# GpSimd waits for VectorE's routing pieces at three rows of each batch of a fused Mamba and mixture-of-experts kernel

## The chip, the cores and the metric

One Trainium2 chip, one core of it. The metric is the device time of one execution in microseconds; several executions are run and the median counts. Lower is better. All arithmetic is float32.

## What is computed

Eight sequences (batches) of 512 tokens with 512 channels go through one Mamba block and then one routed feed-forward layer, each with a residual sum and a layer norm.

```python
xz = einsum('bld,ed->bel', h, in_proj_w)             # 2048 channels: x, z
x = silu(causal_conv4(x) + conv_b)
dt, B, C = split(x_proj(x))                          # rank 32, 16 states, 16 states
delta = softplus(dt @ dt_proj_w.T + dt_proj_b)
state = state * exp(delta * A) + delta * B * x       # over 512 tokens, 1024 x 16 states
y = (sum(state * C) + x * D) * silu(z)
x1 = layernorm(h + y @ out_proj_w.T)

logits = x1 @ gate_w.T                               # 8 experts
top_vals, top_idx = top_k(logits, 2)
w = softmax(top_vals)
out = layernorm(x1 + sum_k w_k * (expert_w[top_idx_k] @ x1 + expert_b[top_idx_k]))
```

## The kernel before

The state of one batch is 16 states times 8 groups of 128 channels, so 128 **rows**, each a scan over 512 tokens. Row `step` is state `n = step // 8` and channel group `j = step % 8`. For each row ScalarE computes the decay `exp(delta*A)` (L1562, `dA`), GpSimd computes the input term `u*B` (L1691, a 128x512 product, written to `hst` or, for `j < 2`, to `first_dbu`), and VectorE scans over both (L1742). After the scans of a state TensorE transposes it (L1152, `hTp`), and VectorE adds it, weighted by C, to `y` (L1731, called a state part here, one before most even rows).

All other work of the layer is cut into named **pieces** and woven between the rows: projections (`x`, `z`, `xproj`, `dt`, `out`), the gather, the routing and the experts of the batch before, and the preparation of the next batch. The function `plan` places each piece in a row of each engine, from costs and due times, when the program is built; the result is a fixed instruction order for each engine, and semaphores hold the engines to each other's results. The batches use these plans: `SEG_PRO` for batch 0, `SEG_TWO` for batch 1, `SEG_FULL` for batches 2 to 6, `SEG_EPI` (scans in halves) for batch 7, and `SEG_LAST` behind it.

The routing of a batch has three pieces on VectorE, all built from small operations:

- `gate` (L1808 to L1823): copy the logits from PSUM, `max` and `max_index` for each of four token tiles, `gap` (L1817, the difference of the two best logits, 128x4), `hit` (L1819) and `hits` (L1823). `hits_ready` rises at its end; `gap_ready` lets ScalarE compute `eg` (L1516).
- `place` (L1838 to L1861): from TensorE's `count` (L1287, L1289, sums over `hits`), the slot of each token and the expert of each tile. `place_ready` rises at its end.
- `route` (L1868 to L1879): the two weights and the matrix `wt`. `wt_ready` rises at its end.

In `SEG_FULL` VectorE has `gate` behind the scan of row 63, `place` behind row 66 and `route` behind row 67; `x0`, `x1`, `x2` (the convolution, L1762, three operations each) follow from row 70 on. GpSimd has, behind its products, `gather1` of tile 3 at row 63, `z4` at row 65, `z5` at 67, `z6` at 70, `z7` at 73 (L1648, each waits for ScalarE's `side`, L1465), the part that is added by a DMA at row 75 (L1668), and `sig0` with `scatter0` at row 75. ScalarE has `eg` at row 65, ahead of `z6`. In `SEG_TWO` the three are behind rows 54, 55 and 56 of VectorE, and GpSimd has `sig0` (L1635) at row 57, `sig1` at 58, `sig2` at 59, three scatters (L1614) at row 60. ScalarE's `sig2` reuses the buffer that GpSimd's `sig0` reads.

GpSimd's product of row r waits for nothing of VectorE but the buffer: for `j < 2` the scan of row r-8, for `j = 2` the transposes of the state before last.

Of the kernel before, what the change touches and what calls it, by code (L numbers as in the profile page):

```python
# [32 lines left out]
ALL_TILES = TILES + HALF_TILES  # L33
LAST_LATE = ALL_TILES - 8
BANKS = 2
SLOTS = 17
USES_BANK = ("z", "zb", "moeL", "den", "countF", "biasF", "out", "outF", "gate", "gateF", "wTF", "count", "wT", "bias", "moe", "x", "xproj", "Ct", "dt")
TURNED = ("yT", "x1T", "xsT", "xsL", "yinit", "yTF", "x1TF")
# [194 lines left out]
def plan(pieces, steps, pace, weave=False):  # L233
# [16 lines left out]
    def ended(x, e, delay=0):  # L250
        if x[0] == "row":
            return not steps or added.get(x[1], 1e9) + delay <= now
        return x[0] not in MAIN and (x, e) not in exists or done.get((x, e), 1e9) + delay <= now
# [44 lines left out]
    def may_start(x):  # L298
# [5 lines left out]
        if x[0] in ("logits", "logF") and x[1] % PAIR:  # L304
            return True
        return len(users) < BANKS or ended((RELEASE[users[-BANKS][0]][0],) + users[-BANKS][1:], RELEASE[users[-BANKS][0]][1], 0.1)

# [56 lines left out]
class Segment:  # L364

    def __init__(self, pieces, pace, blocks, next_blocks, steps=STEPS):
# [10 lines left out]
        self.turned_by = [sum(row < k for row in self.turned_at.values()) for k in range(steps or 1)]  # L377
        assert len(self.use) % BANKS == 0
        self.uses = len(self.use) // BANKS
        self.blocks = blocks + [[] for _ in range(SLOTS - len(blocks))]  # L380
        self.loads = [len(x) for x in self.blocks]
        self.place = {x: (s, k) for s in range(SLOTS) for k, x in enumerate(self.blocks[s])}
        self.after = {x: (self.blocks[s] + next_blocks[s:s + 1])[k + 1:k + 2] for x, (s, k) in self.place.items()}
# [4 lines left out]
def experts(s, tiles):  # L388
    return [("We", k) for k in range(s, tiles, 3)]
# [5 lines left out]
W_FULL = [W_L[s] + W_TWO[s] for s in range(2)]  # L395
KEPT_IN = [[("Wd", e) for e in KEPT if KEPT_SLOTS[e] == s] for s in range(SLOTS)]
W_EPI = [W_L[s] + experts(s, LAST_LATE) for s in range(2)]
W_LATE = [[("Wl", k) for k in range(LAST_LATE, ALL_TILES) if k % 3 == s] for s in range(3)]
GAP = [[]] * 10
GONE_SLOTS = dict(zip(GONE, (10, 11, 4, 5, 8, 9)))  # L400
W_LAST = [W_LATE[min(s, 2)] if s in (0, 1, 14) else [("Wd", e) for e in GONE if GONE_SLOTS[e] == s] for s in range(SLOTS)]

# [80 lines left out]
class When:  # L483
# [13 lines left out]
    def bank(self, piece):  # L497

        k = self.seg.use[piece]
        return k % BANKS, self.bank_base + k // BANKS + 1  # L500

# [38 lines left out]
def periods(engine, period, last):  # L540

    def when(b, segs, before):

        return When({-1: SEG_FIRST, 0: SEG_PRO, 1: SEG_TWO, NB - 1: SEG_EPI, NB: SEG_LAST}.get(b, SEG_FULL), b, b % 2, sum(x.uses for x in segs), sum(len(x.turned) for x in segs),
                    [sum(x.loads[s] for x in segs) for s in range(SLOTS)], before)

# [8 lines left out]
def build(nc, hid, hidT, w_inT, conv_w, conv_b, w_xT, w_dtT, dt_b, A_log, D, w_outT, gateT, w_expT, exp_b, ident_c, before_c, ramp_c, out):  # L555
    with ExitStack() as ctx:
        def sb(name, shape, dt=F32):
            return ctx.enter_context(nc.sbuf_tensor(name, shape, dt))

        def sem(name):  # L560
            return ctx.enter_context(nc.semaphore(name))
# [7 lines left out]
        gate = sb("gate", [P, KD, NE])  # L569
# [54 lines left out]
        place = sb("place", [P, 2, NT, TOP], U32)  # L624
# [74 lines left out]
        def dbu_row(n, j):  # L699

            return first_dbu[:, j, :] if j < 2 else hst[n % 2][:, j, :]
# [3 lines left out]
        hTp = [ctx.enter_context(nc.psum_tensor(f"hTp{s}", [P, DI], F32)) for s in range(2)]  # L705
        bank = [ctx.enter_context(nc.psum_tensor(f"bank{s}", [P, 512], F32)) for s in range(BANKS)]

# [15 lines left out]
        weights_cleared = sem("weights_cleared")  # L723
        w_loaded = [sem(f"w_loaded{s}") for s in range(SLOTS)]
        hidT_in = sem("hidT_in")
# [9 lines left out]
        early_in = [sem(f"early_in{t}") for t in range(NT)]  # L735
        bank_full = [sem(f"bank_full{s}") for s in range(BANKS)]
        bank_taken = [sem(f"bank_taken{s}") for s in range(BANKS)]
# [37 lines left out]
        wt_ready = sem("wt_ready")  # L775
        hits_ready = sem("hits_ready")
        place_ready = sem("place_ready")
# [61 lines left out]
        def all_results(d, slot, halves):  # L839

            _, _, tiles_in = tile_slot(slot)
            return d * (16 * tiles_in) + 16 * (((ALL_TILES if halves else TILES) + 1 - slot) // 2)
# [289 lines left out]
        def _(pe):  # L1132
# [6 lines left out]
            def state_part(b, q, halved, first, turns):  # L1139

                n, _, start = part_of(q, halved)
                per = PAIR if halved else NH
                if q % per == 0:
                    pe.wait_ge(scan_done, b * (NS * ND) + (q // per + 1) * ND)
                if not (first and q < 2):
                    pe.wait_ge(acc_done, sums(b, q - 1))
                if by_dma(q - 2, halved):
                    pe.wait_ge(part_scaled, dma_sums(b, q - 2))
                if not (isinstance(turns, int) and turns == 0):
                    pe.wait_ge(turned_taken, turns)  # L1150
                for j in range(ND):
                    mm = nc.tensor.transpose(hTp[q % 2][:, tok(j)], hst[n % 2][:, j, start:start + P], ident[:, :])  # L1152
                mm.then_inc(hT_done, 1)
# [428 lines left out]
        def _(pool):  # L1582
# [79 lines left out]
            def add_part(w, q):  # L1662

                pool.wait_ge(acc_done, sums(w.b, q + 1 - NH))
                pool.sem_inc(seen_pool, 1)
                pool.wait_ge(part_scaled, dma_sums(w.b, q))
                pool.sem_inc(seen_pool, 1)
                nc.gpsimd.dma_start(y[w.odd][:, q % NH, :], scaled[:, :], accum_op=ALU.add).then_inc(part_added, 16)  # L1668

            def delta_of(w, j):  # L1670
# [5 lines left out]
                pool.wait_ge(xd_ready, w.p * ND + (j + 1))  # L1676
                nc.gpsimd.tensor_tensor(x_j, d, x_j, ALU.mult).then_inc(u_ready, 1)  # L1677

            def period(w):
                for step, pieces in w.rows("pool"):  # L1680
                    n, j = step // ND, step % ND
                    if w.seg.steps and not w.seg.halved and not (w.seg is SEG_PRO and n == 0):
                        if j == 0:
                            pool.wait_ge(b_loaded[n % 2], w.b * (16 * NS // 2) + 16 * (n // 2 + 1))
                        if n == 0:
                            pool.wait_ge(u_ready, w.b * ND + (j + 1))
                        if j < 2 and not (w.seg is SEG_PRO and n == 0):
                            pool.wait_ge(scan_done, w.b * (NS * ND) + ((n - 1) * ND + j + 1))
                        if j == 2 and not (w.seg is SEG_PRO and n < 2):
                            pool.wait_ge(hT_done, w.b * (NS * NH) + (n - 1) * NH)  # L1690
                        nc.gpsimd.tensor_tensor(dbu_row(n, j), u[w.odd][:, j, :], Bbc[n % 2][:, :], ALU.mult).then_inc(dbu_done, 1)  # L1691
                    elif w.seg.halved and j % 2 == 0:
                        k, cols = step // 2, slice(n // NS * HL, (n // NS + 1) * HL)
                        if j == 0:
                            pool.wait_ge(b_loaded[n % 2], w.b * (16 * NS // 2) + 16 * (n // 2 + 1))
                        if n == 0:
                            pool.wait_ge(u_ready, w.b * ND + (j + 2))
                        pool.wait_ge(scan_done, w.b * (NS * ND) + (k // 2 * 6 - 6 if k < 4 else 2 * k - 6))
                        nc.gpsimd.tensor_tensor(half_dbu[k % 4].rearrange("p (k t) -> p k t", k=2), u[w.odd][:, j:j + 2, cols],  # L1699
                                                Bbc[n % 2][:, cols].unsqueeze(1).broadcast_to((P, 2, HL)), ALU.mult).then_inc(dbu_done, 1)  # L1700
                    if w.seg.steps and not w.seg.halved and NH * ((step - 19) // ND) + 2 in BY_DMA and step % ND == 19 % ND:
                        add_part(w, NH * ((step - 19) // ND) + 2)
                    for x in pieces:
                        piece(w, x)
                if w.seg is SEG_PRO:
                    pool.wait_ge(xs_zeroed, 32)

            periods(pool, period, period)


# [252 lines left out]
```

## Time and profile before

| | |
|---|---|
| median of 3 runs | 2321.18 us (2314.91 to 2324.64) |
| the profiled execution | 2323.12 us |
| its span in the trace | 2321.3 us |
| mean granted TensorE clock | 0.927 of full speed |
| instructions | 30421 |

The trace holds one execution. Times are microseconds from the start of the span. PE is TensorE, DVE is VectorE, ACT is ScalarE, POOL is GpSimd. An interval in brackets behind a row is the idle time of that engine before it and what ended it.

### The profile page before, as it was taken

The page shows a single profiled execution, that of the slowest core. Times are in us where ns is not written, and L with a number is a line of the kernel's source. Part 1 is how long each engine was busy: PE and PEld are TensorE (multiplying, and loading weights), DVE is VectorE, ACT ScalarE, POOL GpSimd, SP SyncE. Part 2 cuts the span into 40 slices and gives each one's busy share as a digit, 9 for nine tenths or more (in the row PEclk, how much of TensorE's full clock was granted, in tenths as well). Part 3 has the DMA queues.
Part 4 walks back from the last instruction along what each step waited for, and adds up shares of the span by engine and source line. Part 5 has one row for each costly group of instructions (what it writes and reads, how often), then busy time and mean ns, then how long its engine had stood idle before and what let it go on. Part 6 is the DMA issues. An engine that isn't in the chain of part 4 may idle for free.

```text
span 2321.3 us, 30421 instructions
## 1 busy us (share of the span) xinstructions
PE 2063.1 (89%) x8624; PEld 1226.8 (53%) x8624; DVE 2039.0 (88%) x2191; ACT 1661.8 (72%) x3074; POOL 1850.5 (80%) x1505
## 2 busy tenths in 40 slices
PE   8896779799999989999898989899899998869998
PEld 3444555455564555545555555546555454545543
DVE  5899999999999989998899899999899997989911
ACT  5758858786687948788587876889577885666534
POOL 2959998789987979789797889979797896785603
PEclk9896879899989989899899999999898999869999
DMA  5522143268645785457753687547864576366875
GB/s 175 168 60 78 40 145 103 83 191 285 202 119 167 223 279 146 123 177 255 245 144 100 188 265 241 124 152 233 265 159 127 164 249 232 95 207 225 283 281 118
DMA packets 222085, 412.79 MB, mean 178 GB/s; under 512 B 29880, under 2 KB 36152, under 8 KB 221920
## 3 DMA queue, kind: packets, MB, share of 16 engines
q1 hardware_dynamic: 180448, 322.36, 41.6%
q0 software_dynamic: 20496, 57.16, 12.1%
q10 hardware_dynamic: 20976, 31.33, 4.0%
q8 instruction: 72, 1.18, 0.2%
q14 instruction: 93, 0.76, 0.1%
HBM read 299.37 MB, written 85.72 MB: 166 GB/s over the span
## 4 chain that ended last, share of the span: by engine, by line
POOL 30%; DVE 20%; PE 19%; issue 11%; DMA 10%; ACT 8%; SPq 1%; DVEq 0%; ACTq 0%; POOLq 0%
POOL hst L1691 14%; PE bank L1136 13%; DVE hst L1742 7%; POOL first_dbu L1691 5%; DVE y L1731 4%; PE hTp L1152 4%; DVE u L1762 3%; POOL delta L1674 3%; DMA y<-scaled 3%; POOL u L1677 2%; DMA Bbc<-b_scratch 2%; ACT dA L1562 2%; DVE hst L1907 2%; DVE gap L1817 2%; DMA spare<-gate_scratch 1%
## 5 line engine op out<-in xcount | busy, mean ns | idle before, releaser
L1562 ACT ACTIVATE dA<-delta,negA 128x512 f32<-128x512 f32 (+1 forms) x1146 | 713.4, 637 | 331.5 <-DVE hst L1742 270.7
L1691 POOL TENSOR_TENSOR hst<-u,Bbc 128x512 f32<-128x512 f32 x666 | 875.5, 1431 | 25.6 <-PE hTp L1152 24.9
L1742 DVE TENSOR_TENSOR_SCAN hst<-dA,hst 128x512 f32<-128x512 f32 x672 | 790.3, 1210 | 39.1 <-ACT dA L1562 35.2
L1152 PEld LDWEIGHTS hTp<-ident,hst 128*128 128x128 f32 x4096 | 511.7, 152 | 353.2 <-issue 142.5
L1152 PE MATMUL hTp<-ident,hst 128*128 128x128 f32 x4096 | 575.8, 294 | 130.8 <-DVE y L1731 45.2
L1731 DVE SCALAR_TENSOR_TENSOR y<-hTp,Ct,y 128x1024 f32<-128x1024 f32 x463 | 587.2, 1268 | 75.4 <-PE hTp L1152 59.8
L1691 POOL TENSOR_TENSOR first_dbu<-u,Bbc 128x512 f32<-128x512 f32 x222 | 292.9, 1406 | 4.9 <-DVE hst L1742 2.3
L1742 DVE TENSOR_TENSOR_SCAN hst<-dA,first_dbu 128x512 f32<-128x512 f32 x224 | 263.5, 1210 | 10.8 <-ACT dA L1562 9.7
L1136 PE MATMUL bank<-wslot,hidT 128*128 128x512 f32 x512 | 251.1, 624 | 8.9 <-DMA hidT<-in_hidT 4.3
L1136 PE MATMUL bank<-wslot,tokT 128*128 128x512 f32 x480 | 235.9, 620 | 10.6 <-ACT tokT L1473 10.5
L1136 PE MATMUL bank<-delta,tokT 128*128 128x512 f32 x480 | 226.4, 606 | 0.3 <-issue 0.3
L1136 PE MATMUL bank<-hidT,wslot 128*128 128x512 f32 x384 | 177.7, 601 | 8.3 <-DVE u L1762 8.3
L1762 DVE SCALAR_TENSOR_TENSOR u<-bank,cw,u 128x511 f32<-128x511 f32 (+2 forms) x192 | 142.7, 743 | 28.1 <-ACT u L1386 23.5
L1648 POOL TENSOR_TENSOR zs<-zs,side 128x512 f32<-128x512 f32 x64 | 101.3, 1583 | 68.2 <-ACT side L1465 68.2
L1136 PEld LDWEIGHTS bank<-wslot,hidT 128*128 128x128 f32 x512 | 96.0, 203 | 97.8 <-issue 89.0
L1635 POOL TENSOR_TENSOR u<-u,side 128x512 f32<-128x512 f32 x64 | 84.1, 1315 | 71.6 <-ACT side L1404 71.6
L1136 PEld LDWEIGHTS bank<-wslot,tokT 128*128 128x128 f32 x480 | 88.4, 199 | 99.1 <-issue 94.2
L1136 PEld LDWEIGHTS bank<-delta,tokT 128*128 128x128 f32 x480 | 88.2, 196 | 82.7 <-issue 82.7
L1524 ACT ACTIVATE ysb<-bank 128x512 f32<-128x512 f32 x116 | 68.2, 588 | 84.6 <-PE bank L1136 74.8
L1699 POOL TENSOR_TENSOR first_dbu<-u,Bbc 128x512 f32<-128x512 f32 x64 | 80.2, 1272 | 52.9 <-DMA Bbc<-b_scratch 34.2
L1136 PEld LDWEIGHTS bank<-hidT,wslot 128*128 128x128 f32 x384 | 68.9, 191 | 89.8 <-issue 62.4
L1136 PE MATMUL bank<-wslot,side 128*128 128x512 f32 x240 | 113.3, 600 | 1.7 <-ACT side L1467 1.4
(187 smaller groups left out, 2939.6 us busy)
## 6 DMA issues: line engine op xcount, KB each, us to landing
wslot<-in_w_expT SPq DMA_DIRECT2D x90, 1024.0 KB, 6.9
Bbc<-b_scratch SPq DMA_DIRECT2D x113, 256.0 KB, 3.7
wslot<-in_w_inT SPq DMA_DIRECT2D x26, 1024.0 KB, 5.8
y<-scaled POOLq DMA_DIRECT2D x49, 512.0 KB, 5.3
zs<-sorted_tokens ACTq DMA_DIRECT2D x91, 256.0 KB, 5.3
sorted_results<-ysb SPq DMA_DIRECT2D x90, 256.0 KB, 6.3
res<-in_w_expT SPq DMA_DIRECT2D x18, 1024.0 KB, 6.2
gate_scratch<-zs SPq DMA_DIRECT2D x64, 256.0 KB, 2.0
```

Source lines behind the costliest of these rows:

```text
L1136: mm = nc.tensor.matmul(dst, lhs(k), rhs(k), start=(k == 0), stop=(k == n - 1))
L1152: mm = nc.tensor.transpose(hTp[q % 2][:, tok(j)], hst[n % 2][:, j, start:start + P], ident[:, :])
L1524: nc.scalar.activation(rows, ps[:, :], ACT.Copy).then_inc(bank_taken[s], 1)
L1562: nc.scalar.activation(decay_of(step, halved), delta[w.odd][:, j, cols], ACT.Exp, scale=negA[:, j, n:n + 1]).then_inc(exp_done, 1)
L1635: nc.gpsimd.tensor_tensor(x_j, x_j, side[j % 2][:, :], ALU.mult).then_inc(x_ready, 1)
L1648: nc.gpsimd.tensor_tensor(zs[i % 2][:, :], zs[i % 2][:, :], side[i % 2][:, :], ALU.mult).then_inc(z_ready, 1)
L1674: nc.gpsimd.tensor_tensor(d, d, third(w, j), ALU.add).then_inc(delta_ready, 1)
L1691: nc.gpsimd.tensor_tensor(dbu_row(n, j), u[w.odd][:, j, :], Bbc[n % 2][:, :], ALU.mult).then_inc(dbu_done, 1)
L1699: nc.gpsimd.tensor_tensor(half_dbu[k % 4].rearrange("p (k t) -> p k t", k=2), u[w.odd][:, j:j + 2, cols], Bbc[n % 2][:, cols].unsqueeze(1) ...
L1731: nc.vector.scalar_tensor_tensor(y_part, hTp[q % 2][:, :], Ct[odd][:, t, n:n + 1], y_part, ALU.mult, ALU.add).then_inc(acc_done, 1)
L1742: nc.vector.tensor_tensor_scan(hst[n % 2][:, j, :], dA[j % 2][:, :], dbu_row(n, j), 0.0, ALU.mult, ALU.add).then_inc(scan_done, 1)
L1762: tap = nc.vector.scalar_tensor_tensor(late, bank[s][:, 0:L - k], cw[:, j, TAPS - 1 - k:TAPS - k], late, ALU.mult, ALU.add)
```

## The change

At the head of each row of GpSimd, in batches 1 to 6, the new code looks at the pieces that VectorE's plan has two rows earlier. If one of them is `gate`, `place` or `route`, GpSimd waits until it is done, before the product of this row. So GpSimd waits for `hits_ready` before row 65, for `place_ready` before row 68 and for `wt_ready` before row 69 in `SEG_FULL`, and before rows 56, 57 and 58 in `SEG_TWO`. `SEG_PRO` has none of these pieces, and the halved `SEG_EPI` and `SEG_LAST` are left as they were. Nothing is taken away and no operation is added but the waits: 18 in all.

```diff
+AHEAD = 2
...
+            def stand_back(w, x):
+
+                if x[0] == "gate":
+                    pool.wait_ge(hits_ready, w.e + 1)
+                elif x[0] == "place":
+                    pool.wait_ge(place_ready, w.e + 1)
+                elif x[0] == "route":
+                    pool.wait_ge(wt_ready, w.e + 1)
+
             def period(w):
                 for step, pieces in w.rows("pool"):
                     n, j = step // ND, step % ND
+                    if w.seg.steps and not w.seg.halved and step >= AHEAD:
+                        for x in w.seg.rows["dve"][step - AHEAD]:
+                            stand_back(w, x)
```

## Rows read from the trace of the kernel before

**Rows 1.** The page: busy time by engine, and the chain that ended last.
```profile
PE 2063.1 (89%) x8624; PEld 1226.8 (53%) x8624; DVE 2039.0 (88%) x2191; ACT 1661.8 (72%) x3074; POOL 1850.5 (80%) x1505
...
POOL 30%; DVE 20%; PE 19%; issue 11%; DMA 10%; ACT 8%; SPq 1%; DVEq 0%; ACTq 0%; POOLq 0%
POOL hst L1691 14%; PE bank L1136 13%; DVE hst L1742 7%; POOL first_dbu L1691 5%; DVE y L1731 4%; PE hTp L1152 4%; DVE u L1762 3%; POOL delta L1674 3%; DMA y<-scaled 3%; POOL u L1677 2%; DMA Bbc<-b_scratch 2%; ACT dA L1562 2%; DVE hst L1907 2%; DVE gap L1817 2%; DMA spare<-gate_scratch 1%
```

**Rows 2.** The line of `gap`: shortest, median, longest in ns; first and last start.
```profile
L1817 DVE TENSOR_TENSOR gap<-mx x9: 143/7270/8101, 414.1 to 2241.2; 128x4 f32<-128x4 f32 x7, 128x2 f32<-128x2 f32 x2
```

**Rows 3.** Timeline of VectorE, batch 3: start us, length us, line, operation.
```profile
951.39 8.10 DVE L1817 TENSOR_TENSOR gap<-mx 128x4 f32<-128x4 f32 x1
...
959.79 1.28 DVE L1731 SCALAR_TENSOR_TENSOR y<-hTp,Ct,y 128x1024 f32<-128x1024 f32 x1
...
966.42 0.19 DVE L1838 TENSOR_TENSOR over<-bank,ramp 128x32 f32<-128x32 f32 x1 [0.80 <-PE bank L1289]
...
970.86 0.20 DVE L1861 TENSOR_REDUCE place<-hit_w 128x8 uint32<-128x64 f32 x1
...
974.29 3.44 DVE L1742 TENSOR_TENSOR_SCAN hst<-dA,hst 128x512 f32<-128x512 f32 x3
978.57 1.53 DVE L1762 SCALAR_TENSOR_TENSOR u<-bank,cw,u 128x511 f32<-128x511 f32 x2 [0.84 <-ACT u L1386]
```

**Rows 4.** Timeline of GpSimd in the same stretch of batch 3.
```profile
947.85 3.09 POOL L1691 TENSOR_TENSOR first_dbu<-u,Bbc 128x512 f32<-128x512 f32 x2
950.32 1.84 POOL L1648 TENSOR_TENSOR zs<-zs,side 128x512 f32<-128x512 f32 x1
...
955.22 4.24 POOL L1691 TENSOR_TENSOR hst<-u,Bbc 128x512 f32<-128x512 f32 x3
965.86 1.27 POOL L1648 TENSOR_TENSOR zs<-zs,side 128x512 f32<-128x512 f32 x1 [6.40 <-ACT side L1465]
...
975.24 1.27 POOL L1648 TENSOR_TENSOR zs<-zs,side 128x512 f32<-128x512 f32 x1 [4.32 <-ACT side L1465]
976.47 2.50 POOL L1691 TENSOR_TENSOR hst<-u,Bbc 128x512 f32<-128x512 f32 x2
...
983.43 1.27 POOL L1635 TENSOR_TENSOR u<-u,side 128x512 f32<-128x512 f32 x1 [3.61 <-ACT side L1404]
```

**Rows 5.** Timeline of VectorE in batch 7, `place` from its start to its end.
```profile
2024.17 0.17 DVE L1838 TENSOR_TENSOR over<-bank,ramp 128x32 f32<-128x32 f32 x1
...
2025.62 0.22 DVE L1861 TENSOR_REDUCE place<-hit_w 128x8 uint32<-128x64 f32 x1
```

**Rows 6.** Timeline of TensorE, batch 3, around the routing.
```profile
953.38 2.74 PE L1136 MATMUL bank<-wslot,hidT 128*128 128x512 f32 x6
961.13 1.97 PE L1152 MATMUL hTp<-ident,hst 128*128 128x128 f32 x8 [5.01 <-DVE y L1731]
962.89 1.71 PE L1287 MATMUL bank<-hits,ones 128*128 128x8 f32 x8
```

**Rows 7.** Timeline of TensorE, batch 7: `count` from its first to its last group.
```profile
2022.01 0.96 PE L1287 MATMUL bank<-hits,ones 128*128 128x8 f32 x8
...
2023.05 0.81 PE L1289 MATMUL bank<-hits,ones 128*128 128x24 f32 x6
```

**Rows 8.** Stretches: length; busy PE, PEld, DVE, ACT, POOL; granted clock, DMA share, GB/s.
```profile
951.40:973.10 21.70, 16.69 (x57) 11.66 (x56) 20.63 (x26) 10.83 (x26) 13.12 (x11) 0.72 0.13 49
...
951.40:1225.80 274.40, 250.47 (x1075) 149.45 (x1074) 251.18 (x251) 206.93 (x373) 235.13 (x192) 0.95 0.62 189
```

**Rows 9.** Timeline of batch 1: GpSimd's first `sig`, first scatter, then a pair of scans.
```profile
408.28 1.27 POOL L1635 TENSOR_TENSOR u<-u,side 128x512 f32<-128x512 f32 x1 [6.25 <-ACT side L1404]
...
428.34 1.07 POOL L1614 DMA_INDIRECT sorted_tokens<-tokT,place  x1 [4.73 <-ACT tokT L1512]
...
434.93 2.33 DVE L1742 TENSOR_TENSOR_SCAN hst<-dA,hst 128x512 f32<-128x512 f32 x2
```

**Rows 10.** The chain in order of time, batch 3: start us, length us, link.
```profile
1087.96 9.76 DMA y<-scaled
```

## The prediction

> **What bounds the kernel now.** I read the page first. Three engines are nearly full, TensorE 89%, VectorE 88%, GpSimd 80% [rows 1], and the chain that ended last passes from one to another: GpSimd owns 30% of it, VectorE 20%, TensorE 19%. No engine is the bound alone. So a time saved counts only if the chain runs through it. The reader should look at the last entries of that chain: `gap`, a 128x4 subtraction, has 2% of it, some 46 us by the rounded share. The view of its line says why: nine of them, the shortest 0.143 us, the median 7.27 us, the longest 8.10 us [rows 2]. A 50-fold spread for one shape is no work, it is something that holds the operation. I then read the timelines of VectorE and GpSimd side by side around it. In batch 3 `gap` starts at 951.39 and ends at 959.49 [rows 3]. GpSimd works without a pause from 947.85 on, and its last product of that run ends at 955.22 + 4.24 = 959.46 [rows 4], 0.03 us before `gap` does. Seven GpSimd operations pass while `gap` stands. The other four batches on the same plan show the same picture, with 7.27 to 8.08 us.
>
> Why does the run end there? GpSimd's next piece waits for ScalarE's `side`, 6.40 us [rows 4], and ScalarE has `eg`, which needs `gap`, ahead of it. So GpSimd holds `gap` until it has run as far ahead as it can, and then it waits itself. TensorE too stands 5.01 us, for VectorE's state part behind `gap` [rows 6], and its granted clock over 951.4 to 973.1 is 0.72 against 0.95 for the whole batch [rows 8]. So the hold stops all four engines: this is lost time, not covered time.
>
> `place` is held in the same way but less: in batch 3 from 966.42 to 971.06, 4.64 us [rows 3]; in batch 7, where GpSimd is mostly quiet, from 2024.17 to 2025.84, 1.67 us [rows 5].
>
> **The change part by part, batches 2 to 6.** I lay out the new order for batch 3, with durations from the rows. *Before row 65.* GpSimd did rows 64 and 65 from 947.85, 1.23 us apart, so it now stops at about 949.1. `gap` is ready at 951.39 as before and finds GpSimd idle: 0.14 us instead of 8.10, a gain of 7.96. `hit` and `hits` follow, done at about 951.95. GpSimd goes on 2.9 us later than it would have. VectorE's state part starts at 959.79 - 7.96 = 951.83, scan 64 at 953.0, scan 65 at 954.1. Row 65's product is done at 953.3, just in time: cover of 0.8 us.
>
> *Row 66 and `place`.* The next state part needs transposes that TensorE starts after its own work, which ends at 953.38 + 2.74 = 956.1 [rows 6]. Eight took 1.97 us at the lower clock, so I give them half of it, some 0.9 to 1.0; so the part starts at 957.0 rather than 955.3: 1.75 us of the gain turn into a wait for TensorE. `count` follows at 957.0 and takes 2023.05 + 0.81 - 2022.01 = 1.85 us [rows 7], so it is done at 958.9; now it takes from 962.89 to about 966.3 at the lower clock, and VectorE waits 0.80 us for it [rows 3, 6]. Scan 66 ends at 959.3, so this 0.80 is gone. Meanwhile GpSimd does 65, `z4`, 66, 67 and `z5`, five operations of 1.23, and stands at row 68 from 958.2. `place` runs with GpSimd quiet from 959.3 in 1.67 us instead of 4.64: a gain of 2.9 and an end at 961.0. GpSimd stood another 2.8 us.
>
> *`route`.* Scan 67 runs to 962.1. GpSimd has begun row 68's product at 961.0 and stops before row 69. So `route` now meets a running product, which it does not today. That can cost it between 0 and one product, 1.23; the held operations in today's `place` lose about 1 us each, and I take 0.9. GpSimd loses about 0.8 waiting for `wt_ready`.
>
> *Sum for one batch:* 7.96 - 1.75 + 0.80 + 2.9 - 0.9 = 9.0 us.
>
> **Who could be late next.** GpSimd has three new waits, 2.9 + 2.8 + 0.8 = 6.5 us. Queued behind them are rows 65 to 75, `z4` to `z7`, and the part added by DMA; ScalarE's `z6` waits for `z4`, VectorE's scans for the products. Against that stand two waits of today, 6.40 and 4.32 [rows 4], both for a ScalarE that is itself held by VectorE and so comes some 9 us earlier. From `wt_ready` at about 963.2 GpSimd has rows 69 to 75 with `z6` and `z7`, nine operations of 1.23: it ends row 75 at 974.3, against 976.47 + 2.50 = 978.97 today. That is 4.7 earlier while VectorE is 9 earlier; the lead shrinks. But behind it GpSimd waits 3.61 for `sig0` [rows 4], and VectorE has the long convolution pieces there [rows 3]. So it catches up to within a microsecond. TensorE has between 956.1 and its first `x` only transposes, `count` and eight matmuls, some 7 us; it is on time with about 1 us to spare.
>
> After this stretch nothing in the batch is tied to a time outside it: the rest of the chain (GpSimd's run, the wait of 9.76 us for the DMA that adds a part [rows 10]) starts with it, and the next `gate` comes as much earlier. TensorE is busy 250.5 of 274.4 us of the batch [rows 8], part of it at the lower clock; in 265 us that is 95%, high but possible. The five batches give 5 x 9.0 = 45 us. Bounds: at most 7.96 + 0.80 + 2.9 = 11.7 each, 58 in all; at least nothing, were another engine to take it all.
>
> **Batch 1.** Here `gap` is held for 1.08 us only, and `place` loses two holds of about 1 us, so VectorE has some 3 us to win. But GpSimd waits much longer, because these waits stand before rows that it does early today: rows 56 and 57 are done before 402, and `sig0` at 408.28 [rows 9]. With the waits, row 57 follows `place_ready` at about 421.8 and `sig0` ends at 424.3. ScalarE's `sig2` needs that buffer, and behind it in ScalarE's queue stand the decay of row 57 and `x3`. GpSimd itself reaches the first scatter at about 432.3 instead of 428.34 [rows 9], 4.0 late, and it has no pause for 30 us from there. Its lead over the scans at row 61 is 2.8 us today (product done at 433.3, scan due at 436.1, the second of the pair at 434.93 [rows 9]), so VectorE comes 1.2 to 2 us late. I take a loss of 2, between a gain of 1 and a loss of 4.
>
> Batch 7 and the end aren't touched and only come earlier. To issue the 18 waits I cost at nothing: GpSimd's products follow each other at 1.23 us with the waits that they have, and each new wait stands where GpSimd has to stop anyway.
>
> **The sum.** 45 - 2 = 43 us. From the profiled execution's 2323.1 us this makes 2280.1, from the median, which is 1.9 lower, 2278.2. I predict **2278 us**, 1.9% faster.
>
> **A rule against it.** `gap` stands for seven GpSimd operations, while three scans, which also read two SBUF tensors, run at 1.15 us each beside products [rows 3, 4]. The Trainium skill, "SBUF — State Buffer", in its section "SBUF: two separate sides", says that the pair of ports that VectorE and GpSimd share is an exclusive lock, held for one whole instruction, and that the other is blocked until it ends. By that rule `gap` could lose one product and not seven, and the rest of the 8 us would have another cause. The sum would then be 2303 us and not 2278. The rows agree that something is exclusive (`gap` ends with GpSimd's run) but not on how long.
>
> **Rivals.**
> - *One product each.* If GpSimd holds a small operation for one product only and something else keeps `gap`, each batch wins 1.2 for `gap` and 2.9 for `place`: 5 x 4.1 - 2 = 18.5, 2303 us. Against it: the end of `gap` within 0.03 us of GpSimd's last product. 4%. (It is what the rule of the Trainium skill's "SBUF — State Buffer" would make of this kernel.)
> - *Half given back.* TensorE or GpSimd, both over 85% busy in a batch, take up about half of the gain downstream: 5 x 4.5 - 2 = 20.5, 2300 us. For it: cover of only 0.8 us at row 65 and 1 us on TensorE. 14%.
> - *No net effect.* `gap` gets its 8 us back and another cycle of the batch, for instance the DMA waits in its second half, keeps the pace; or the waits fall so that GpSimd is working again when `gap` comes. 2310 to 2330 us, about 2320. Against it: the chain goes through `gap`. 8%.
> - *Slower.* GpSimd's own queue becomes the bound: the two waits for `side` stay as long and 6.5 us a batch come on top. 5 x 6.5 + 4 = 36.5, 2358 us. The point is the end of row 75's product: it decides against the change once that lies over 27.6 us behind the start of `gap` (978.97 - 951.39), and I expect 22.9. For it: GpSimd's 30% of the chain. 6%.
> - *The forecast,* 2262 to 2292 us: 68%.
>
> **How the numbers follow.** A measurement of this kernel can tell about 0.5% from no change, 11.6 us. The forecast, the half and the single product are faster by more: 86%. No net effect 8%, slower 6%. The range takes in the forecast with its bounds (58 us less at most, which is 2263) and the half with a little spread: 2262 to 2303, 82%.
>
> **What would show it.** Right: five `gap` of batches 2 to 6 at 0.14 to 0.2 us; `place` in 1.7 to 2 us; GpSimd's waits at L1691 before rows 65, 68 and 69 of some 3, 3 and 1 us; no wait of 5 us of TensorE for `y`, a granted clock near 1 in this stretch; the distance from one `gate` to the next near 264 us. Wrong: `gap` short and that distance still 272; scans that wait for GpSimd's products behind row 65; `route` held for more than one product; in batch 1 a delay of more than 4 us at the scatters.

## The result, and the profile after

The changed kernel takes 2284.38 us (median, 2282.69 to 2292.98) against 2320.75 us for the kernel before: ratio 0.9853, 95% interval 0.982 to 0.9886. That is 36 us or 1.5% less; 2278 us was forecast, in a range of 2262 to 2303. The profiled execution has a span of 2281.1 us, 40.2 less than the span before.

The page of the changed kernel, the same lines as [rows 1] (lines of `kernel.py` behind the new function are 13 higher, those between 36 and it one higher; `gap` is L1830, the product L1704, the scan L1755):

```profile
PE 2037.1 (89%) x8624; PEld 1201.8 (53%) x8624; DVE 1983.3 (87%) x2191; ACT 1660.2 (73%) x3074; POOL 1850.8 (81%) x1505
...
POOL 25%; PE 10%; issue 9%; DMA 7%; DVE 7%; ACT 3%; SPq 1%; ACTq 0%; DVEq 0%; POOLq 0%
```

VectorE is busy 55.7 us less with the same 2191 instructions, and TensorE 26.0 us less with the same 8624, at a mean granted clock of 0.941 where it was 0.927. GpSimd's busy time hasn't changed. `gap` is gone from the chain. Its line, and what GpSimd's products now wait for (us, times):

```profile
L1830 DVE TENSOR_TENSOR gap<-mx x9: 142/146/148, 413.5 to 2201.7; 128x4 f32<-128x4 f32 x7, 128x2 f32<-128x2 f32 x2
```
```profile
  DVE hits L1836: 29.2, 6
  PE hTp L1153: 26.9, 17
  DVE place L1874: 15.7, 6
  DVE wt L1892: 6.4, 6
```

The longest `gap` is now 0.148 us where the median was 7.27 [rows 2]. Batch 3 again, VectorE, GpSimd and TensorE, to be read beside [rows 3, 4, 6]:

```profile
947.72 0.15 DVE L1830 TENSOR_TENSOR gap<-mx 128x4 f32<-128x4 f32 x1
...
951.67 1.26 DVE L1744 SCALAR_TENSOR_TENSOR y<-hTp,Ct,y 128x1024 f32<-128x1024 f32 x1
...
953.98 0.17 DVE L1851 TENSOR_TENSOR over<-bank,ramp 128x32 f32<-128x32 f32 x1
...
955.48 0.22 DVE L1874 TENSOR_REDUCE place<-hit_w 128x8 uint32<-128x64 f32 x1
955.61 1.21 DVE L1755 TENSOR_TENSOR_SCAN hst<-dA,hst 128x512 f32<-128x512 f32 x1
956.74 0.33 DVE L1881 TENSOR_SCALAR den<-eg 128x4 f32<-128x4 f32 x1
```
```profile
942.59 1.57 POOL L1630 DMA_INDIRECT ysb<-sorted_results,place  x1 [0.16 <-issue]
943.60 1.86 POOL L1704 TENSOR_TENSOR first_dbu<-u,Bbc 128x512 f32<-128x512 f32 x1
948.40 1.27 POOL L1704 TENSOR_TENSOR first_dbu<-u,Bbc 128x512 f32<-128x512 f32 x1 [2.94 <-DVE hits L1836]
...
955.78 1.26 POOL L1704 TENSOR_TENSOR hst<-u,Bbc 128x512 f32<-128x512 f32 x1 [1.18 <-DVE place L1874]
958.07 2.51 POOL L1704 TENSOR_TENSOR hst<-u,Bbc 128x512 f32<-128x512 f32 x2 [1.03 <-DVE wt L1892]
...
966.68 2.51 POOL L1704 TENSOR_TENSOR hst<-u,Bbc 128x512 f32<-128x512 f32 x2
```
```profile
948.03 2.74 PE L1137 MATMUL bank<-wslot,hidT 128*128 128x512 f32 x6
950.61 1.04 PE L1153 MATMUL hTp<-ident,hst 128*128 128x128 f32 x8
```

The reader should see three things. The three waits of GpSimd are there, 2.94, 1.18 and 1.03 us. The waits that it had for ScalarE's `side`, 6.40 and 4.32, are gone. And the 5.01 us in which TensorE stood for VectorE are gone too. The whole batch, as in [rows 8], from one `gap` to the next:

```profile
947.70:1209.90 262.20, 241.28 (x1070) 142.99 (x1069) 240.35 (x250) 206.47 (x373) 235.17 (x191) 0.98 0.64 198
```

It is 262.2 us long instead of 274.4. The distances between the starts of `gap`, in both kernels:

```text
from gap of batch      1 to 2   2 to 3   3 to 4   4 to 5   5 to 6   6 to 7   7 to the end
before                 266.1    271.2    274.4    272.0    273.1    249.8    300.6
changed                271.3    262.9    262.2    262.4    263.1    243.6    302.0
```

From batch 2 on these five distances are 46.3 us shorter. The first is 5.2 longer (the first `gap` itself is 0.6 earlier), the last 1.4 longer: 46.3 - 5.2 + 0.6 - 1.4 = 40.3.

### The profile page after: what moved, and what is told of

Its sections match the earlier page's. It is cut to its first block, busy times and chain, and to the rows that moved or that the text cites. A ratio compares the mean times of both kernels' runs of the same rounds, so it can differ in the third digit from the quotient of the medians.

```text
span 2281.1 us, 30428 instructions
## 1 busy us (share of the span) xinstructions
PE 2037.1 (89%) x8624; PEld 1201.8 (53%) x8624; DVE 1983.3 (87%) x2191; ACT 1660.2 (73%) x3074; POOL 1850.8 (81%) x1505
## 3 DMA queue, kind: packets, MB, share of 16 engines
q8 instruction: 72, 1.18, 0.2%
## 4 chain that ended last, share of the span: by engine, by line
POOL 25%; PE 10%; issue 9%; DMA 7%; DVE 7%; ACT 3%; SPq 1%; ACTq 0%; DVEq 0%; POOLq 0%
POOL hst L1704 12%; PE bank L1137 8%; POOL first_dbu L1704 4%; DMA y<-scaled 2%; DVE hst L1755 2%; DVE y L1744 2%; POOL delta L1675 2%; POOL u L1678 2%; DVE hst L1920 1%; DMA Bbc<-b_scratch 1%; POOL ysb L1630 1%; DVE u L1775 1%; PE hTp L1153 1%; POOL zs L1649 1%; ACT dA L1563 1%
## 5 line engine op out<-in xcount | busy, mean ns | idle before, releaser
L1704 POOL TENSOR_TENSOR hst<-u,Bbc 128x512 f32<-128x512 f32 x666 | 870.7, 1412 | 42.3 <-PE hTp L1153 26.9
L1755 DVE TENSOR_TENSOR_SCAN hst<-dA,hst 128x512 f32<-128x512 f32 x672 | 791.0, 1211 | 50.9 <-ACT dA L1563 46.9
L1153 PEld LDWEIGHTS hTp<-ident,hst 128*128 128x128 f32 x4096 | 498.3, 149 | 325.6 <-issue 140.4
L1153 PE MATMUL hTp<-ident,hst 128*128 128x128 f32 x4096 | 560.1, 288 | 106.0 <-DVE hst L1755 33.7
L1704 POOL TENSOR_TENSOR first_dbu<-u,Bbc 128x512 f32<-128x512 f32 x222 | 292.9, 1393 | 42.0 <-DVE hits L1836 29.2
L1755 DVE TENSOR_TENSOR_SCAN hst<-dA,first_dbu 128x512 f32<-128x512 f32 x224 | 263.3, 1210 | 9.5 <-ACT dA L1563 7.0
L1137 PE MATMUL bank<-wslot,hidT 128*128 128x512 f32 x512 | 244.3, 610 | 10.4 <-ACT zs L1459 5.0
L1137 PE MATMUL bank<-delta,tokT 128*128 128x512 f32 x480 | 220.8, 593 | 0.0
L1649 POOL TENSOR_TENSOR zs<-zs,side 128x512 f32<-128x512 f32 x64 | 95.6, 1493 | 15.2 <-ACT side L1466 15.2
```

What stands on the lines that cost most here:

```text
L1137: mm = nc.tensor.matmul(dst, lhs(k), rhs(k), start=(k == 0), stop=(k == n - 1))
L1649: nc.gpsimd.tensor_tensor(zs[i % 2][:, :], zs[i % 2][:, :], side[i % 2][:, :], ALU.mult).then_inc(z_ready, 1)
L1755: nc.vector.tensor_tensor_scan(hst[n % 2][:, j, :], dA[j % 2][:, :], dbu_row(n, j), 0.0, ALU.mult, ALU.add).then_inc(scan_done, 1)
```

## Experiments

The theory that went into them: GpSimd's run holds VectorE's small operation, and the change pays by taking GpSimd out of the way. Open were how long one GpSimd operation can hold, whether it is `gap` itself that is special, which of the three waits pays, whether batch 1 loses, and what GpSimd's standing costs. All variants below put their waits into batches 2 to 6 unless said otherwise.

### What holds gap: a short pause behind the last gather

```diff
                     n, j = step // ND, step % ND
+                    if w.seg is SEG_FULL and step == 64:
+                        pool.wait_ge(scan_done, w.b * (NS * ND) + 64)
```

> The kernel before, with one wait in batches 2 to 6 that has nothing to do with routing: GpSimd's product of row 64 waits for VectorE's scan of row 63, a pause of about 1.4 us that is over before gap starts; GpSimd then runs on through gap. Theory (gap is held until GpSimd's run ends, however it began): gap 7 to 9.5 us, time 2320 to 2328 us. Rival (what matters is the overlapped state of GpSimd's run, where operations start every 1.23 us and last 1.8; a pause ends that state, and then an operation holds for one product only): gap at most 1.3 us, some 7 us less in each of five batches, about 2288 us.

Measured: 2296.25 us, ratio 0.9872 (0.9829 to 0.9915); `gap` 0.34 to 0.85 us in the five batches. GpSimd and VectorE in batch 3:

```profile
945.02 1.57 POOL L1629 DMA_INDIRECT ysb<-sorted_results,place  x1 [0.16 <-issue]
947.09 2.49 POOL L1693 TENSOR_TENSOR first_dbu<-u,Bbc 128x512 f32<-128x512 f32 x2 [0.50 <-DVE hst L1744]
949.54 1.33 POOL L1648 TENSOR_TENSOR zs<-zs,side 128x512 f32<-128x512 f32 x1
950.84 2.50 POOL L1693 TENSOR_TENSOR hst<-u,Bbc 128x512 f32<-128x512 f32 x2
```
```profile
949.27 0.34 DVE L1819 TENSOR_TENSOR gap<-mx 128x4 f32<-128x4 f32 x1
...
956.97 1.34 DVE L1846 TENSOR_TENSOR_SCAN end<-ones,tiles 128x8 f32<-128x8 f32 x1
958.34 1.18 DVE L1848 TENSOR_TENSOR begin<-end,tiles 128x8 f32<-128x8 f32 x1
959.45 1.41 DVE L1849 TENSOR_TENSOR past<-ramp,end 1x120 f32<-1x120 f32 x1
```

The first theory falls: a pause of 0.50 us (1.0 to 1.4 in the other four batches), over before `gap` starts, frees it while GpSimd works right on. The difference stands in GpSimd's lengths. Before, an operation in this run lasts 1.8 us though the next starts 1.23 us after it [rows 4], so two always overlap by 0.6 and GpSimd is never between operations. Behind the pause one lasts 1.27 and touches the next by 0.04. Then a small operation of VectorE waits only for the rest of the one that runs. `place` isn't helped: five of its operations now meet a busy GpSimd, and it takes 6.8 us (956.53 to 963.36) instead of 4.64. From the start of `gap` to VectorE's first convolution operation (`x0`) it is 22.4 us in the mean of the five batches, where it was 27.0: 5 x 4.6 = 23 us. Beside the kernel before, taken again with it (2319.56), the time fell by 23.3. So a pause that has nothing to do with the routing gives about two thirds of what the change gives.

### What sets the overlap up: the same pause ahead of the gather

```diff
+                    if w.seg is SEG_FULL and step == 63:
+                        pool.wait_ge(scan_done, w.b * (NS * ND) + 62)
```

> The kernel before with one short wait in batches 2 to 6, ahead of GpSimd's product of row 63 (for VectorE's scan of row 61), so about 1 us of pause as in short_pause, but ahead of the gather that follows this product. Theory (a product right behind a DMA that GpSimd issues starts some 0.6 us before the end of it, the overlap is handed on from product to product until a pause, and while it lasts VectorE's small operation never gets in): the gather sets the overlap up again, gap stays at 7 to 9 us, time near 2320 us. Rival (any pause of GpSimd in these rows is enough, or the shift against VectorE is): gap below 1.3 us, about 2296 us as short_pause.

Measured: 2323.21 us, ratio 1.0012 (0.9985 to 1.0038); `gap` 8.57 to 8.60 us.

```profile
949.12 1.28 POOL L1693 TENSOR_TENSOR hst<-u,Bbc 128x512 f32<-128x512 f32 x1 [0.83 <-DVE hst L1744]
950.55 1.57 POOL L1629 DMA_INDIRECT ysb<-sorted_results,place  x1
951.56 3.08 POOL L1693 TENSOR_TENSOR first_dbu<-u,Bbc 128x512 f32<-128x512 f32 x2
954.01 1.85 POOL L1648 TENSOR_TENSOR zs<-zs,side 128x512 f32<-128x512 f32 x1
```

The pause ended the overlap, as the 1.28 us of the product shows. The gather behind it set it up again: it ends at 952.12, and the product starts at 951.56, 0.56 us before that. Every following operation inherits this until the run ends. So it takes two things to hold `gap` for 8 us: a gather issued by GpSimd with a product right behind it, and no pause since. It isn't any DMA of GpSimd: in the kernel before, the product behind each of the 40 gathers into `ysb` starts 0.53 to 0.63 us before the gather's record ends, while behind the scatters (`sorted_tokens`) it starts 0.02 us or more after the end. What in the chip makes the overlap isn't shown; the runs show that the long hold comes and goes with it.

### Which operation is held

`gap` is taken out, ScalarE computes `exp` of the difference from the two logits.

```diff
-                    nc.vector.tensor_tensor(gap[:, ts], mx[:, ts, 1], mx[:, ts, 0], ALU.subtract).then_inc(gap_ready, 1)
                     dve.wait_ge(step_done, base + 2 * n)
+                    dve.sem_inc(gap_ready, 1)
...
-                    nc.scalar.activation(eg[:, first:end_t], gap[:, first:end_t], ACT.Exp).then_inc(eg_ready, 1)
+                    for t in range(first, end_t):
+                        done = nc.scalar.activation(eg[:, t:t + 1], mx[:, t, 0:1], ACT.Exp, scale=-1.0, bias=mx[:, t, 1:2])
+                    done.then_inc(eg_ready, 1)
```

> The kernel before without the operation gap: ScalarE computes exp(second best - best) from the two logits itself in four small operations, so VectorE's next operation is hit, which also reads two SBUF tiles. No wait is added. Theory (GpSimd's overlapped run holds whichever small operation with two SBUF inputs comes first): hit takes 7 to 8 us instead of 0.21, time about as before, 2316 to 2322 us. Rival (something about gap itself, its strided reads of mx right behind max_index): hit stays at 0.2 us and the time falls by 30 to 40 us.

Measured: 2322.88 us, ratio 0.9998 (0.9972 to 1.0023). The line of `hit`, and the end of GpSimd's run in batch 3:

```profile
L1821 DVE TENSOR_TENSOR hit<-ramp,mi x9: 191/7486/7978, 416.9 to 2244.9; 128x64 f32<-128x64 f32 x7, 128x32 f32<-128x32 f32 x2
```
```profile
955.84 7.49 DVE L1821 TENSOR_TENSOR hit<-ramp,mi 128x64 f32<-128x64 f32 x1
```
```profile
959.00 4.24 POOL L1693 TENSOR_TENSOR hst<-u,Bbc 128x512 f32<-128x512 f32 x3
```

`hit` took 0.21 us before and inherits the hold: it ends at 963.33, GpSimd's run at 963.24. What is held is the next small operation that can be held, not `gap` as such. To save `gap` would have saved nothing.

### Which wait pays

```diff
# gate_only
                 if x[0] == "gate":
                     pool.wait_ge(hits_ready, w.e + 1)
# place_only
                 if x[0] == "place":
                     pool.wait_ge(place_ready, w.e + 1)
# no_route: both of these, without the wait for wt_ready
```

> Batches 2 to 6, the wait for hits_ready before row 65 alone; no wait for place or route. Theory (each wait pays by what it frees on VectorE): gap 0.15 us, place again 3.5 to 4.6 us instead of 1.7, so 5 x 2.9 = 14 us above the kernel with all three waits in batches 2 to 6, about 2294 us. Rival (GpSimd's time counts as well): the two waits left out gave it back 1.2 + 1.0 us a batch, and the two cancel, about 2280 to 2284 us.

Measured: 2300.83 us, ratio 0.9911 (0.9879 to 0.9943); `gap` 0.15 us. `place` took 5.8 us in batch 3 (955.34 to 961.15), longer than today and than expected, because GpSimd no longer waits for ScalarE there and is busy all through it. Without its two waits `place` costs VectorE 4 us a batch and not 2.9, and `route` 0.9 us. In time the theory's figure holds: 12.6 us above the kernel with all three waits in the same batches (2288.21, full_only below) where 14 was expected, and the two intervals just don't overlap (from 0.9879 and up to 0.9877). The rival, that the two waits give nothing, falls.

> Batches 2 to 6, the wait for place_ready before row 68 alone. GpSimd then stops at 955.2 (behind z5) in the times of before, while gap is held. Theory (gap ends when GpSimd stops): gap about 3.9 us, place 1.7 us, some 6.5 us won a batch, about 2288 us. Rival (gap is held by ScalarE or DMA work and GpSimd's stop is chance): gap stays near 8 us, place alone wins 2.9 a batch, and GpSimd stands until place is done, about 2306 us or worse.

Measured: 2293.86 us, ratio 0.9861 (0.9818 to 0.9904); `gap` 3.2 to 4.4 us. Batch 3:

```profile
954.98 3.68 DVE L1826 TENSOR_TENSOR gap<-mx 128x4 f32<-128x4 f32 x1
```
```profile
956.82 1.82 POOL L1649 TENSOR_TENSOR zs<-zs,side 128x512 f32<-128x512 f32 x1
966.45 3.72 POOL L1700 TENSOR_TENSOR hst<-u,Bbc 128x512 f32<-128x512 f32 x3 [7.82 <-DVE place L1870]
```

`gap` ends at 958.66 and GpSimd's shortened run at 958.64. The wait for `place` pays twice: it ends the run over `gap` as well. GpSimd stood 7.82 us for that, and the batches still came out shorter.

> Batches 2 to 6 with the waits for hits_ready and place_ready, without the one for wt_ready. Theory (single products hold a small operation for what is left of them, and only den and mix in route can be held): route 1.3 to 2.5 us instead of 1.3, GpSimd 1.0 us earlier a batch, the two cancel: equal to the kernel with all three waits, 2280 to 2288 us. Rival (route's operations are held for 1.2 us each as those of place were): 5 x 3 us slower, 2298 us.

Measured: 2286.99 us, ratio 0.9849 (0.9782 to 0.9916). `route` took 3.1 us in all five batches, where it takes 1.25 in four of the five in the changed kernel and 1.06 undisturbed; 2.5 was the most I had expected. The time doesn't tell it from the changed kernel. 1.8 us of VectorE and 1.0 us of GpSimd are traded: `x0` comes 18.7 us behind the start of `gap` in the mean, against 17.5 in full_only, and whether GpSimd's lead gives that back later can't be told.

### How long GpSimd's waits may be, and where they may stand

```diff
# full_only: the three waits, AHEAD = 2, in batches 2 to 6 only
-                    if w.seg.steps and not w.seg.halved and step >= AHEAD:
+                    if w.seg is SEG_FULL and step >= AHEAD:
# ahead1, ahead3: full_only and
-AHEAD = 2
+AHEAD = 1        (3 in ahead3)
# pause_place: the pause of short_pause, and the wait for place_ready before row 68
```

> The changed kernel with the waits one row behind VectorE's pieces instead of two (before rows 64, 67 and 68), batches 2 to 6. Theory (GpSimd's cover for the scans is some 0.8 us): gap 0.15 and place 1.7 us as before, but scan 67 comes 1.3 us late for its product and scans 64 and 65 by 0.2 to 0.4, so 5 x 1.5 to 2 us slower than the waits two rows behind: about 2290 to 2294 us. Rival (GpSimd has lead to spare): within 2 us of it, 2284 us.

Measured: 2300.14 us, ratio 0.9885 (0.9835 to 0.9935). GpSimd stood 4.68, 4.51 and 1.16 us in batch 3, 10.4 together against 5.2 in the changed kernel, and `den` came 2.80 us behind `place` instead of 1.26: scan 67 was 1.5 us late for its product, as expected. The gain of `gap` and `place` is there, and by the medians (2288.21 for full_only, below) a third of the whole is lost again. The intervals of the two overlap (0.9835 to 0.9935 and 0.979 to 0.9877), so the trace has to carry this: `x0` comes 19.5 us behind the start of `gap` in the mean, against 17.5, which makes 10 us in five batches. GpSimd's standing is free only while its products still come in time.

> Batches 2 to 6, all three waits, one row later than in the changed kernel (before rows 66, 69 and 70). GpSimd then still does row 65 and z4, overlapped, when gap comes. Theory (an overlapped run holds gap until its last operation ends): gap 0.6 to 1.2 us, place 1.7 us, GpSimd stands less; 2284 to 2290 us. Rival (the lead of GpSimd was short in the changed kernel): 5 us faster than it, 2279 us.

Measured: 2275.22 us (2269.30 to 2278.47), ratio 0.9797 (0.973 to 0.9864), the fastest median of all and below the figures of both theories. `gap` took 0.15 to 1.01 us, in batch 3 0.72 (to 949.81, with the end of `z4`, 947.92 + 1.87 = 949.79). So the hold to the end of an overlapped run is seen once more. GpSimd stood 3.9 us.

> Batches 2 to 6 with two waits, for hits_ready before row 66 and for place_ready before row 69; no wait for route. It takes the placing of ahead3 and leaves out its wait for wt_ready, 1.0 us of GpSimd a batch. Theory (with the overlap gone, GpSimd's standing time is the only price left, and ahead3 is 0.5% below the changed kernel because GpSimd stands 1.3 us less a batch): ratio to the kernel before 0.976 to 0.982, 2268 to 2278 us. Rival (the 9 us between ahead3 and the changed kernel are the spread between runs): ratio 0.983 to 0.987, about 2285 us.

Measured: 2284.82 us, ratio 0.9836 (0.9805 to 0.9867): the rival's figure. Leaving the third wait out shows no gain, and the 9 us between ahead3 and the changed kernel aren't shown to be a gain. The two intervals overlap (0.973 to 0.9864, 0.982 to 0.9886). In the traces the distances between the five `gap` and the next differ by 15 us, and only 3 of it lie where the waits act: `x0` comes 16.9 us behind the start of `gap` in ahead3 and 17.4 in the changed kernel, five times 0.57. The other 12 lie behind `x0`, where the two kernels don't differ. Whether AHEAD = 3 is better than 2 stays open.

> Batches 2 to 6: the short pause of short_pause ahead of row 64 instead of the wait for hits_ready, and the wait for place_ready before row 68; no wait for route. Theory (the overlap costs the 8 us, single products cost about 1.2 each): gap 0.3 to 1.1 us, place 1.7 us instead of the 6.6 of short_pause, so 5 x 4.5 us below short_pause less what GpSimd stands, about 2278 to 2284 us, equal to the changed kernel or a little below. Rival (GpSimd's lead is what counts): GpSimd comes to row 68 earlier and stands longer, no better than 2290 us.

Measured: 2284.18 us, ratio 0.9815 (0.9764 to 0.9866); `gap` 0.47 to 0.67 us, `place` 1.7 us. GpSimd's pause for `gap` fell from 2.94 to 1.10 us, but it stood 3.72 for `place` instead of 1.18: it only came sooner to the next wait. The median is the theory's, at its upper end, but the four executions reach from 2272.95 to 2305.43, which takes in the rival's 2290, and the trace is of the slowest of them.

### Batch 1

> The changed kernel with the waits in batches 2 to 6 alone; batch 1 is as before. Theory (batch 1 loses): the second gap came 684.81 - 680.18 = 4.6 us later in the changed kernel, so this one comes 4 to 5 us below it, about 2280 us, with gap of batch 2 back near 680. Rival (the delay of batch 1 is caught up later on): within 1 us of the changed kernel, 2284 us.

Measured: 2288.21 us (2279.7 to 2293.75), ratio 0.9833 (0.979 to 0.9877). The median speaks for neither theory, and the spread takes in both. From `gap` of batch 1 to that of batch 2 it took 271.0 us, as long as in the changed kernel (271.3), though this batch has no new wait. That distance alone can't show a loss.

```diff
# two_only: the three waits in batch 1 alone
+                    if w.seg is SEG_TWO and step >= AHEAD:
```

> The three waits in batch 1 alone (before rows 56, 57 and 58). Theory (they cost more than they give there): in batch 1 the first scatter comes 4.2 us later behind gap than today (20.1 instead of 14.2 to 15.9 us), the last bias piece 2 to 4 us later, and the time is 2 to 5 us above the kernel before, 2323 to 2327 us, which a run cannot tell from no change. Rival (batch 1 gains its 3 us from gap and place): the last bias piece not later, 2317 us.

Measured: 2326.06 us, ratio 1.0018 (0.9987 to 1.0049), no difference that a run can tell. The trace of batch 1, GpSimd:

```profile
415.66 1.27 POOL L1704 TENSOR_TENSOR first_dbu<-u,Bbc 128x512 f32<-128x512 f32 x1 [15.25 <-DVE hits L1836]
422.64 1.28 POOL L1704 TENSOR_TENSOR first_dbu<-u,Bbc 128x512 f32<-128x512 f32 x1 [5.71 <-DVE place L1874]
...
433.40 1.07 POOL L1615 DMA_INDIRECT sorted_tokens<-tokT,place  x1 [0.18 <-issue]
```

The first scatter comes 18.4 us behind the start of `gap`, and 20.1 in the changed kernel. In the traces where batch 1 is as before it comes after 14.0 to 18.3 us, and the last bias piece of VectorE (L1887, `res`) after 66.7 to 70.4 us against 69.0 and 71.1 with the waits. These ranges nearly meet or overlap, so the figures have to be compared like with like: `place` itself starts 5.7 to 8.9 us behind `gap` where GpSimd has no new wait at all. In us:

```text
place starts behind gap at     first scatter   last bias piece   kernels
5.9, no waits in batch 1       14.2            67.0 to 67.3      before, pause_early, gate_only, no_route, ahead3_no_route
5.9, with the waits            18.4            69.0              two_only
7.6, no waits in batch 1       15.9            68.9              short_pause, full_only
7.6, with the waits            20.1            71.1              changed
```

So the waits of batch 1 delay GpSimd's first scatter by 4.2 us and VectorE's last bias piece by about 2. Whether anything of it reaches the end can't be told from the spread between executions.

## Why the prediction was right, step by step

- **GpSimd holds `gap`, and it is on the chain: right, but the mechanism was half told.** I wrote that GpSimd holds it until it has run as far ahead as it can. The end did coincide, but what makes the hold so long is the overlap behind a gather. A pause of 0.5 us would have done (short_pause). With the words of the first sum, "finds GpSimd idle", the 7.96 us came out right: 8.10 became 0.15.
- **The rule against it.** The Trainium skill, "SBUF — State Buffer", section "SBUF: two separate sides", says that the lock is held for one whole instruction. The runs agree with this wherever GpSimd's operations merely touch: `begin` and `past` in short_pause last 1.18 and 1.41 us. They go beyond it where the operations overlap: seven of them hold as one. So the rule, read word for word, isn't what this case shows, and the measurement decides. That the overlapped operations hold the ports as one unbroken occupation is my reading of it; no run shows the lock itself.
- **`place` 4.64 to 1.67: right**, 1.72 us measured (953.98 to 955.70). GpSimd's waits came out at 2.9, 1.2 and 1.0 where I had 2.9, 2.8 and 0.8. The second is shorter by the step that follows.
- **1.75 us of waiting for TensorE: wrong.** I let the state part behind scan 65 wait for the eight transposes that follow TensorE's six matmuls [rows 6]. It doesn't need them: its own were made earlier. The state part starts 3.95 us behind the start of `gap` in all five batches, not the 5.6 that I had. Batch 5 of the changed kernel decides it, for there the transposes start 1.85 us after the state part. What comes late there is `count`, and with it `place`:

```profile
1476.25 1.26 DVE L1744 SCALAR_TENSOR_TENSOR y<-hTp,Ct,y 128x1024 f32<-128x1024 f32 x1
...
1480.93 0.19 DVE L1851 TENSOR_TENSOR over<-bank,ramp 128x32 f32<-128x32 f32 x1 [2.29 <-PE bank L1290]
```
```profile
1478.10 1.04 PE L1153 MATMUL hTp<-ident,hst 128*128 128x128 f32 x8
1478.97 0.96 PE L1288 MATMUL bank<-hits,ones 128*128 128x8 f32 x8
```

- **When `count` is done: forecast 1.9 us too late for four batches, too early for one.** I had 7.5 us behind the start of `gap`; it is 5.6 in batch 3. The matmuls and transposes ahead of the six in [rows 6] had run at half clock (0.50, the lower of the two levels, 1.2 GHz), and I took their times as they were. Before the change:

```profile
949.00:951.00 2.00, 2.00 (x12) 1.48 (x12) 1.06 (x10) 1.75 (x4) 2.00 (x3) 0.74 0.91 130
951.00:953.40 2.40, 2.40 (x11) 1.78 (x10) 2.40 (x6) 1.37 (x4) 2.40 (x3) 0.51 0.23 67
```

  In the changed kernel the clock stays at 1.00 over the same work in batch 3 (946.0 to 950.6). In its batch 5 it is at 0.50 there (1472.0 to 1475.5), VectorE waits 2.29 us for `count`, and `place` starts 8.6 us behind `gap` instead of 6.3. That the clock was up in four of the five is luck: in full_only, with the same waits in these batches, it is at half there in all five, and `place` starts 7.2 to 8.3 us behind `gap`.
- **`route` held for 0.9: too much**, 0.2 us (`den` 0.33 instead of 0.13), since GpSimd's one product began 0.17 us behind scan 67.
- **Next late: none of the engines that I feared by much.** Row 75's product ended at 969.19, 21.5 us behind the start of `gap`; 22.9 was forecast and 27.6 was the point of the slower rival. VectorE's `x0` did start later than its own work allowed: scan 70 waited 1.18 us for a decay of ScalarE, and `x0` 1.09 us for its input where it had waited 0.84. ScalarE wasn't in my list of who could be late.

```profile
962.61 1.23 DVE L1755 TENSOR_TENSOR_SCAN hst<-dA,hst 128x512 f32<-128x512 f32 x1 [1.18 <-ACT dA L1563]
```

- **The five batches: 46.3 us measured, 45 forecast; that they are so close is luck.** Up to `x0` the sum of batch 3 closes: 7.95 + 0.80 + 2.9 - 0.2 - 1.2 - 0.25 = 10.0 us, and `x0` comes 17.2 us behind the start of `gap` instead of 27.2. The mean of the five batches is 9.6 us here and 9.5 in full_only, where 9.0 was forecast. So this part is solid, though the misses (+1.75 for TensorE, +0.7 for `route`, -1.4 for ScalarE) partly cancel. Behind `x0` it isn't: there the five batches take 1207 us in the changed kernel and 1217 in full_only, and 1197 to 1208 in the four traces without new waits in these batches (before, pause_early, no_gap, two_only). By full_only's trace the five distances are 36 us shorter and not 46. Whether some of the gain is given back downstream, as the second rival has it, these traces can't tell.
- **Batch 1: a loss of 2 forecast.** The trace shows 4.6 up to the next `gap`, but the runs with an unchanged batch 1 spread by as much (265.7 to 271.0 us), so this figure is not shown. Compared like with like the forecast holds as far as batch 1 can be followed: 4.0 late at the first scatter was forecast and 4.2 found, 2 for VectorE and 1.7 to 2.2 found at the last bias piece.
- **The end: 1.4 us longer**, which I had at nothing and didn't study.
- **The median moved 36 and not 43 us.** The profiled execution moved 40. The rest lies within the spread between executions; the four of the changed kernel lie within 10 us of each other. By the interval of the ratio it is 26 to 42 us less, which doesn't quite reach the 43.

## What to carry to other kernels

A tiny operation whose length varies 50-fold is waiting, not working: put the other engine's timeline beside it and look at whose run ends when it ends. If that run consists of operations that last longer than the distance between their starts, a short pause behind the DMA that sets this up frees the other engine, and it needs no long wait. (To move the DMA instead was not tried.) Ask of such a hold which operation comes first behind it, since removing that one only passes the hold on; and place a wait so that the stopped engine's results still come in time, for one row earlier was 12 us slower here by the medians (2300 against 2288, with intervals that overlap) and 10 us by the traces.

## What the runs showed of the hardware that I had not expected

- A GpSimd product that is issued right behind a gather of GpSimd starts 0.53 to 0.63 us before the end of the gather's record (40 of 40 in the kernel before), and the operations behind it keep this overlap (1.8 us long, 1.23 us apart) until GpSimd waits for something. Behind the DMA that adds a part (`y<-scaled`) the overlap is 0.06 to 0.43 us where nothing was waited for; behind a scatter there is none. While the long overlap lasts, `gap` and `hit`, small VectorE operations with two SBUF inputs, are held to the end of the run: 8.10 us for seven operations, 3.68 and 0.72 us where the run was cut shorter.
- Two SBUF inputs aren't needed to be held. In the kernel before, the last but one operation of `place` has a single one and takes 1.24 us beside a GpSimd product, against 0.15 in the changed kernel:

```profile
969.70 1.24 DVE L1858 TENSOR_SCALAR tile_expert<-owner 1x15 int32<-1x15 f32 x1
```

- The large scans aren't held though both of their inputs lie in SBUF: in the kernel before, 672 of them last between 1.195 and 1.228 us, with GpSimd busy 80% of the time. The scan over 8 elements in `place` is held (0.17 us in the changed kernel, 1.34 in short_pause). Why the large ones escape was not tried.

```profile
L1742 DVE TENSOR_TENSOR_SCAN hst<-dA,hst x672: 1195/1214/1228, 61.6 to 1919.5; 128x512 f32<-128x512 f32 x168
```

- TensorE's granted clock can fall to 0.50 (1.2 GHz, the lower level) at the end of the 32 small matmuls of `gate` or right behind it, with TensorE busy before and after, and it can stay at 1.00 over the same work. Behind `gate` it is at half in four of batches 2 to 6 in the kernel before (not in batch 4), in one in the changed kernel (batch 5) and in all five in full_only. Where it falls, `place` starts 1.0 to 2.4 us later in the changed kernel and in full_only. It is one part of the spread between executions. What decides it was not found.
